# Two of sixteen low halves of the probabilities, made by GpSimd instead of VectorE, in a two-layer cross-attention kernel

## The chip, the cores and the metric

The kernel runs on one core of a Trainium2 chip. The metric is the device time of one execution in microseconds (us), lower is better. The engines are named as in the profile: PE is TensorE (PEld its weight loads), DVE is VectorE, ACT is ScalarE, POOL is GpSimd, SP is SyncE, which here only starts DMA transfers.

## The reference

The input x has 8 batches of 512 rows and 512 columns. It goes through two layers. Each layer adds to x a cross-attention over 77 context rows, and then a feed-forward product, each on a layer-normalised x.

```
x = x + xattn0(layernorm(x), ctx, mask)     # 16 heads of 32, softmax over 77 keys
x = x + ffn0(layernorm(x))                  # rows quantised to 8 bits, ternary weights
x = x + xattn1(layernorm(x), ctx)           # 16 heads of 64, output projection Wo
x = x + ffn1(layernorm(x))                  # FFT, sparse product, inverse FFT: one 512x512 matrix
```

Inside an attention:

```
scores = einsum('bhqd,bhkd->bhqk', q, k) / sqrt(HD)
probs = softmax(scores, axis=-1)
ctx = einsum('bhqk,bhkd->bqhd', probs, v)
```

## The kernel before

Every value that a matmul reads is kept as two fp16 numbers, a high half (the value rounded) and a low half (what the rounding left), and a product is made of three matmuls (lines 150 to 152). After a setup of about 195 us the batches go through a software pipeline: iteration i runs in 18 slots, and within it the stages work on different batches. Stage X is the first layer's attention (batch i), Y the second layer's attention (batch i-1), Z its output projection and second feed-forward (batches i-2, i-3), W the queries of the next batch. In the steady state an iteration takes 114 us.

An attention is cut into 8 units of 128 rows by 8 heads. X units 0 to 7 have their scores in slots 0 to 7, Y units 0 to 7 in slots 10 to 17, so slots 8 and 9 have no unit of their own. A unit that belongs to slot u goes on as follows. In slot u DVE takes the row maxima (`maxima`), ACT the exponential (`exp`), in fp32, into the tile `pr`. In slot u+1 DVE makes the reciprocals of the sums (`sums`, tile `sm`), and POOL multiplies `pr` by them in place (`normalise`, line 939). In slot u+2 ACT writes the high half, 256 times `pr`, in fp16 into the tile `ph` (`probs_high`, line 995), DVE writes the low half, 256 times `pr` minus the high half, beside it (`probs_low`, line 1156), and SP starts the transposing DMA of both into `prT` (`turn`), which PE reads for the product with the values. For X unit 6 that is slot 8 and for X unit 7 slot 9.

Each engine has its own list of work, written slot by slot in the same order, and meets the others by semaphores alone. Within a slot the orders are:

- DVE: maxima, sums of the unit before, the low halves of what PE's fills left in PSUM (`low`: `lo_part` at lines 1086 and 1088, `add_to` at line 1095 with the layernorm sums), `probs_low`, in slot 8 the layernorm sums of the next batch (`ln0`, lines 1037 to 1053), and then what the table `LOWER` lists: `quantise` or `rows_low`. In slot 9 that is `quantise` of layernorm 1 (lines 1062 to 1070), which makes the 8-bit rows of the first feed-forward.
- ACT: the high halves of the fills (line 963), `probs_high`, what `APPLY` lists (`ln_apply`, lines 1007 and 1010), `exp`. In slot 10 that is `ln_apply` of layernorm 3. It writes the buffers `xh` and `xn` and so waits until the last DVE step of `quantise` of slot 9 (line 1070) is done.
- POOL: `normalise`, then `rstd_of` for every layernorm group whose sums end in this slot (lines 930 and 932; in slot 8 that of `ln0`, which waits for DVE's line 1053), then what `BIAS` lists (`add_bias`, two additions at line 945). In slot 7 and in slot 10 there is such a pair.
- SP: `turn`, `turn_rows`, then stores and loads; in slot 8 four loads of `k0b` stand behind the `turn` of X unit 6.
- PE: in each slot the scores of the next unit, then the fills. In slots 8 to 11 these are the queries of Y (`project`), the value products of X rows 2 and 3, and the first feed-forward product. The scores of Y unit 2 wait for the exponential of Y unit 0.

The units in `HEADWISE` (X 7 and Y 0 among them) get their sums from ACT's exponential, so DVE's `sums` is for them the reciprocal alone.

Of the kernel before, what the change touches and what calls it, by code (L numbers as in the profile page):

```python
# [24 lines left out]
CH = (GK + 2) // 3  # L25
# [81 lines left out]
LN0_STATS = 8  # L107
HEADWISE = {("X", 0), ("X", 2), ("X", 5), ("X", 7), ("Y", 0), ("Y", 2), ("Y", 3), ("Y", 5)}
ROWS_BY_DVE = {(2, 2)}
APPLY = {2: [(2, 2)], 8: [(1, 0)], 10: [(3, 0)], 11: [(0, 0)], 12: [(0, 2)], 13: [(1, 2)], 14: [(3, 2)], 16: [(2, 0)]}  # L110
LOWER = {2: [(2, 2)], 9: [(1, 0)], 10: [(3, 0)], 11: [(0, 0)], 12: [(0, 2)], 13: [(1, 2)], 15: [(3, 2)], 17: [(2, 0)]}
BIAS = {7: [(2, 2)], 10: [(1, 0)], 12: [(3, 0)], 14: [(1, 2)], 17: [(2, 0), (3, 2)]}
# [22 lines left out]
def listed(table, g):  # L135

    i, s = SLOTS[g]
    out = [(j, pair, i - ln_lag(j, pair)) for j, pair in table.get(s, [])]
    return [e for e in out if there(e[2])]
# [602 lines left out]
def layers(nc, k, x, scr_k0, scr_k1, scr_v0, scr_v1, out):  # L742

    here = ExitStack()
    with here:
# [164 lines left out]
        def _(pool):  # L910
# [13 lines left out]
            def rstd_of(j, t0, width, b):  # L924
                n = GROUPS[j, b, t0]
                ts = slice(t0, t0 + width)
                pool.wait_ge(ln_var, n + 1)
                if b > 0:
                    pool.wait_ge(ln_applied, APPLIED[j, t0 + width - 2, b - 1] + 1)
                pool.tensor_tensor(rstd[:, j, ts], var[:, j, ts], mhalf[:, ts], ALU.pow).then_inc(rstd_ready, 1)  # L930
                pool.wait_ge(rstd_ready, n + 1)
                pool.tensor_tensor(shift[:, j, ts], mean[:, j, ts], rstd[:, j, ts], ALU.mult).then_inc(ln_ready, 1)  # L932

            def normalise(stage, u, b):
                U = UNIT[stage, u, b]
                pool.wait_ge(sums_ready, U + 1)
                v = pr[U % 3][:, :, 0:GK].rearrange("p g (h n) -> p g h n", h=4)
                s = sm[:, U % 4, :].rearrange("p (g h u) -> p g h u", g=2, u=1).broadcast_to([P, 2, 4, KEYS])
                pool.tensor_tensor(v, v, s, ALU.mult).then_inc(probs_ready, 1)  # L939

            def add_bias(j, pair, b):
                pool.wait_ge(ln_lowered if (j, pair) in ROWS_BY_DVE else ln_applied, APPLIED[j, pair, b] + 1)
# [5 lines left out]
            for g, (i, s) in enumerate(SLOTS):  # L948
                if unit_at(g - 1):
                    normalise(*unit_at(g - 1))  # L950
                for e in groups_at(g):
                    rstd_of(*e)
                for e in listed(BIAS, g):
                    add_bias(*e)

        @block.scalar
        def _(act):
# [31 lines left out]
            def probs_high(stage, u, b):  # L989
                U = UNIT[stage, u, b]  # L990
                act.wait_ge(probs_ready, U + 1)
                if U >= 2:
                    before = [v for v in UNIT if UNIT[v] == U - 2][0]
                    act.wait_ge(turned[before[1]], 16 * (PASS[before] + 1))
                act.activation(ph[:, U % 2, 0, :, :, 0:CH], pr[U % 3][:, :, 0:GKP].rearrange("p g (c n) -> p g c n", c=3), ACT.Copy,  # L995
                               scale=PS).then_inc(probs_hi, 1)

            def ln_apply(j, pair, b):
                n = APPLIED[j, pair, b]
# [32 lines left out]
        def _(dve):  # L1032
# [113 lines left out]
            def sums(stage, u, b):  # L1146
                U = UNIT[stage, u, b]
                dve.wait_ge(exp_done, U + 1)
                if (stage, u) not in HEADWISE:
                    step(dve.tensor_reduce(sm[:, U % 4, :].rearrange("p (g h) -> p g h", g=2), four(pr[U % 3][:, :, 0:GK]), AX.X, ALU.add))  # L1150
                dve.reciprocal(sm[:, U % 4, :], sm[:, U % 4, :]).then_inc(sums_ready, 1)  # L1151

            def probs_low(stage, u, b):
# [12 lines left out]
            for g, (i, s) in enumerate(SLOTS):  # L1166
# [3 lines left out]
                    sums(*unit_at(g - 1))  # L1170
                for use in SLOT_DRAINS[g]:
                    low(use)
                if unit_at(g - 2):
                    probs_low(*unit_at(g - 2))
                if s == LN0_STATS and there(i + 1):
                    ln0(i + 1)
# [205 lines left out]
```

## Time and profile before

| | us |
|---|---|
| median of 3 runs | 1245.94 (1243.89 to 1248.01) |
| the profiled execution, its own time | 1248.5 |
| its span, first to last instruction | 1246.7 |
| busy in it: PE | 975.0 (78%) |
| busy in it: DVE | 949.6 (76%) |
| busy in it: ACT | 647.6 (52%) |
| busy in it: POOL | 401.9 (32%) |

The span covers the setup, the pipeline's filling and emptying, and the iterations between. A share of busy time says little here: the stages have different limits, and what counts is, in each stretch, which engine is waited for last. "Idle before" at the end of a row is how long the engine stood before this instruction, and which instruction's end let it go on. Instruction ends on PE are modelled, and rows on POOL are rough.

### The profile page before, as it was taken

To read this page: it belongs to the slowest core of one execution; us is meant where nothing else is said; L and a number is where in the kernel's file an instruction comes from. 1 tells how busy PE (TensorE), PEld (TensorE's weight loads), DVE (VectorE), ACT (ScalarE), POOL (GpSimd) and SP (SyncE) were. 2 spreads that over 40 slices of the span, in tenths; PEclk is the share of its full clock that TensorE was granted. 3 is DMA by queue.
4 is the path that set the end of the run, shared out by engine and by line. 5 is a ranking of instruction groups with operands and counts; after the bars stand their busy time and mean duration, and the time that the engine had idled before them with its cause. 6 is when DMAs were issued, how large, how long until landed. Compare 5 with 4: busy or idle time off the path is not lost. (4 is left out here: it accounts for less than half of the span.)

```text
span 1246.7 us, 17114 instructions
## 1 busy us (share of the span) xinstructions
PE 975.0 (78%) x6020; PEld 511.7 (41%) x6020; DVE 949.6 (76%) x1740; ACT 647.6 (52%) x1658; POOL 401.9 (32%) x351
## 2 busy tenths in 40 slices
PE   3989950455587796999699879969996998789694
PEld 1446430232254343445345444444453444335341
DVE  5798973286879969987996999699888968944722
ACT  1334340363657648754964686387548646613701
POOL 0011004041433334523442444345234424511402
PEclk9999985756788798999899979989997999699797
DMA  9412332163555565575658465755745563550512
GB/s 343 164 34 70 115 119 91 34 128 68 90 114 109 102 115 93 108 133 114 110 103 155 76 121 102 150 100 99 140 106 115 101 119 65 113 102 17 106 47 68
DMA packets 374983, 132.83 MB, mean 107 GB/s; under 512 B 364753, under 2 KB 367345, under 8 KB 371442
## 3 DMA queue, kind: packets, MB, share of 16 engines
q1 hardware_dynamic: 374898, 131.74, 50.1%
q8 instruction: 48, 0.79, 0.3%
q14 instruction: 37, 0.30, 0.1%
HBM read 35.91 MB, written 16.11 MB: 42 GB/s over the span
## 5 line engine op out<-in xcount | busy, mean ns | idle before, releaser
L939 POOL TENSOR_TENSOR pr<-pr,sm 128x616 f32<-128x616 f32 x128 | 169.3, 1322 | 449.7 <-DVE sm L1151 449.7
L982 ACT ACTIVATE pr<-scores,mx,factor 128x77 f32<-128x77 f32 x512 | 203.9, 419 | 42.9 <-DVE mx L1139 42.8
L150 PE MATMUL wb<-xT,wq_hl 128*128 128x512 f16 x384 | 150.8, 393 | 68.1 <-DMA xT<-xh 68.1
L151 PE MATMUL wb<-xT,wq_hl 128*128 128x512 f16 x384 | 150.3, 391 | 0.0
L152 PE MATMUL wb<-xT,wq_hl 128*128 128x512 f16 x384 | 149.5, 389 | 0.0
L995 ACT ACTIVATE ph<-pr 128x618 f16<-128x618 f32 x128 | 92.6, 723 | 103.0 <-DMA prT<-ph 90.2
L150 PE MATMUL scores<-k1b,qc 128*128 128x154 f16 x256 | 62.5, 261 | 88.8 <-ACT pr L982 88.0
L1156 DVE SCALAR_TENSOR_TENSOR ph<-pr,ph 128x618 f16<-128x618 f32 x128 | 125.9, 983 | 3.7 <-ACT ph L995 3.7
L930 POOL TENSOR_TENSOR rstd<-var,mhalf 128x2 f32<-128x2 f32 (+1 forms) x48 | 52.6, 1096 | 179.9 <-DVE var L1053 172.8
L982 ACT ACTIVATION_READ_ACCUMULATOR pr<-scores,mx,factor 128x1 f32 x512 | 107.2, 209 | 0.0
L1136 DVE TENSOR_REDUCE mx<-scores 128x8 f32<-128x616 f32 x128 | 101.3, 791 | 6.3 <-PE scores L152 6.1
L150 PE MATMUL wb<-wo_hl,qc 128*128 128x512 f16 x256 | 97.0, 379 | 7.1 <-DVE qc L1086 6.8
L152 PE MATMUL wb<-wo_hl,qc 128*128 128x512 f16 x256 | 97.0, 379 | 0.0
L151 PE MATMUL wb<-wo_hl,qc 128*128 128x512 f16 x256 | 97.0, 379 | 0.0
L1079 DVE TENSOR_TENSOR xh<-xn,xh 128x1024 f16<-128x1024 f32 x48 | 73.4, 1530 | 30.4 <-ACT xn L1010 30.0
L1095 DVE SCALAR_TENSOR_TENSOR xr<-wb,factor,xr 128x512 f32<-128x512 f32 x48 | 35.7, 744 | 76.9 <-PE wb L152 76.9
L1007 ACT ACTIVATE xh<-xr,shift,rstd 128x512 f16<-128x512 f32 x72 | 57.9, 812 | 56.0 <-POOL shift L932 33.3
L150 PEld LDWEIGHTS wb<-xT,wq_hl 128*128 128x128 f16 x384 | 38.8, 101 | 114.0 <-issue 74.5
L963 ACT ACTIVATE qc<-wb,bq_s 128x512 f16<-128x512 f32 x64 | 42.3, 686 | 79.6 <-PE wb L152 79.6
L1010 ACT ACTIVATE xn<-xr,shift,rstd 128x512 f32<-128x512 f32 x84 | 66.9, 810 | 11.7 <-POOL shift L932 10.3
L945 POOL TENSOR_TENSOR xr<-xr,bf_b 128x512 f32<-128x512 f32 x48 | 69.9, 1476 | 3.8 <-ACT xn L1010 3.8
L1224 PE MATMUL scores<-mrow,ones 128*128 128x308 bf16 x128 | 42.0, 328 | 36.0 <-ACT pr L982 32.4
(178 smaller groups left out, 2571.6 us busy)
## 6 DMA issues: line engine op xcount, KB each, us to landing
xr<-in_x SPq DMA_DIRECT2D x6, 1024.0 KB, 5.7
out_x<-xr SPq DMA_DIRECT2D x6, 1024.0 KB, 5.4
a_dft_kf<-in_dft SPq DMA_DIRECT2D x1, 3072.0 KB, 14.2
a_stage<-in_wk SPq DMA_DIRECT2D x3, 1024.0 KB, 5.7
a_stage<-in_wv SPq DMA_DIRECT2D x3, 1024.0 KB, 5.6
scr_v<-a_wq_vs SPq DMA_DIRECT2D x1, 2560.0 KB, 7.8
scr_k<-a_wo_ks SPq DMA_DIRECT2D x1, 2464.0 KB, 7.2
k1b<-scr_k SPq DMA_DIRECT2D x16, 154.0 KB, 6.7
```

Source lines behind the costliest of these rows:

```text
L150: pe.matmul(out, lhs(0), rhs(0), start=start, stop=False, **kw)
L151: pe.matmul(out, lhs(0), rhs(1), start=False, stop=False, **kw)
L152: return pe.matmul(out, lhs(1), rhs(0), start=False, stop=stop, **kw)
L939: pool.tensor_tensor(v, v, s, ALU.mult).then_inc(probs_ready, 1)
L945: ins = pool.tensor_tensor(xs(b)[:, t, :], xs(b)[:, t, :], k[bias][:, :], ALU.add)
L982: ins = act.activation(pr[U % 3][:, h // 4, cols], sc[:, U % 2, h // 4, cols], ACT.Exp, bias=mx[:, U % 4, h:h + 1], scale=k["factor"][:, f ...
L995: act.activation(ph[:, U % 2, 0, :, :, 0:CH], pr[U % 3][:, :, 0:GKP].rearrange("p g (c n) -> p g c n", c=3), ACT.Copy, scale=PS).then_inc( ...
L1007: ins = act.activation(xh[:, n % 2, t - pair, 0, :], xs(b)[:, t, :], ACT.Identity, bias=shift[:, j, t:t + 1], scale=rstd[:, j, t:t + 1])
L1010: ins = act.activation(xn[:, t - pair, :], xs(b)[:, t, :], ACT.Identity, bias=shift[:, j, t:t + 1], scale=rstd[:, j, t:t + 1])
L1079: dve.tensor_tensor(xh[:, n % 2, :, 1, :], xn[:, :, :], xh[:, n % 2, :, 0, :], ALU.subtract).then_inc(ln_lowered, 1)
L1136: step(dve.tensor_reduce(m, s, AX.X, ALU.max))
L1156: dve.scalar_tensor_tensor(out=ph[:, U % 2, 1, :, :, 0:CH], in0=pr[U % 3][:, :, 0:GKP].rearrange("p g (c n) -> p g c n", c=3), scalar=PS, ...
```

## The change

The set `LOW_BY_POOL` names X units 6 and 7. For these two:

- DVE no longer runs `probs_low`; POOL runs it, in the same slot (8 and 9), behind `normalise` and `rstd_of` and ahead of `add_bias`. POOL's form is a plain subtraction without the factor 256.
- The factor moves: DVE divides the sums by 256 ahead of the reciprocal (a tensor_scalar on 128x8, with a wait between the two), so that `pr` comes out of `normalise` 256 times as large, and ACT's `probs_high` uses the scale 1.
- `rstd_of` gets a further wait on DVE's `ln_lowered` of the batch before, for the second group of layernorm 2.

```diff
+LOW_BY_POOL = {("X", 6), ("X", 7)}
...
                 pool.wait_ge(ln_var, n + 1)
                 if b > 0:
                     pool.wait_ge(ln_applied, APPLIED[j, t0 + width - 2, b - 1] + 1)
+                    for pair in range(t0, t0 + width, 2):
+                        if (j, pair) in ROWS_BY_DVE:
+                            pool.wait_ge(ln_lowered, APPLIED[j, pair, b - 1] + 1)
...
+            def probs_low(stage, u, b):
+                U = UNIT[stage, u, b]
+                pool.wait_ge(probs_hi, U + 1)
+                pool.tensor_tensor(ph[:, U % 2, 1, :, :, 0:CH], pr[U % 3][:, :, 0:GKP].rearrange("p g (c n) -> p g c n", c=3),
+                                   ph[:, U % 2, 0, :, :, 0:CH], ALU.subtract).then_inc(probs_lo, 1)
...
                 for e in groups_at(g):
                     rstd_of(*e)
+                if unit_at(g - 2) and unit_at(g - 2)[:2] in LOW_BY_POOL:
+                    probs_low(*unit_at(g - 2))
                 for e in listed(BIAS, g):
                     add_bias(*e)
...
                 act.activation(ph[:, U % 2, 0, :, :, 0:CH], pr[U % 3][:, :, 0:GKP].rearrange("p g (c n) -> p g c n", c=3), ACT.Copy,
-                               scale=PS).then_inc(probs_hi, 1)
+                               scale=1.0 if (stage, u) in LOW_BY_POOL else PS).then_inc(probs_hi, 1)
...
                     step(dve.tensor_reduce(sm[:, U % 4, :].rearrange("p (g h) -> p g h", g=2), four(pr[U % 3][:, :, 0:GK]), AX.X, ALU.add))
+                if (stage, u) in LOW_BY_POOL:
+                    step(dve.tensor_scalar(sm[:, U % 4, :], sm[:, U % 4, :], 1.0 / PS, None, ALU.mult))
                 dve.reciprocal(sm[:, U % 4, :], sm[:, U % 4, :]).then_inc(sums_ready, 1)
...
-                if unit_at(g - 2):
+                if unit_at(g - 2) and unit_at(g - 2)[:2] not in LOW_BY_POOL:
                     probs_low(*unit_at(g - 2))
```

POOL in slots 7 to 10 of one iteration, before. `pr<-pr,sm` is `normalise` of X unit 7, the rows on 128x4 are `rstd_of` for `ln0`, `bf_b` is the bias that `add_bias` adds.

```order
L945 TENSOR_TENSOR xr<-xr,bo_b 128x512
L939 TENSOR_TENSOR pr<-pr,sm 128x2x308 [waits sums_ready]
L930 TENSOR_TENSOR rstd<-var,mhalf 128x4 [waits ln_applied,ln_var]
L932 TENSOR_TENSOR shift<-mean,rstd 128x4 [waits rstd_ready]
L945 TENSOR_TENSOR xr<-xr,bf_b 128x512 [waits ln_applied]
L945 TENSOR_TENSOR xr<-xr,bf_b 128x512
```

The same place after:

```order
L955 TENSOR_TENSOR xr<-xr,bo_b 128x512
L943 TENSOR_TENSOR pr<-pr,sm 128x2x308 [waits sums_ready]
L934 TENSOR_TENSOR rstd<-var,mhalf 128x4 [waits ln_applied,ln_var]
L936 TENSOR_TENSOR shift<-mean,rstd 128x4 [waits rstd_ready]
L948 TENSOR_TENSOR ph<-pr,ph 128x6x103 [waits probs_hi] x2
L955 TENSOR_TENSOR xr<-xr,bf_b 128x512 [waits ln_applied]
L955 TENSOR_TENSOR xr<-xr,bf_b 128x512
```

Both low halves now stand one behind the other between `rstd_of` and the two additions.

DVE from the end of slot 7 to `quantise` in slot 9, before. `ph<-pr,ph` are `probs_low` of X units 5, 6 and 7, and `amax`, `cscale`, `ascale` belong to `quantise`.

```order
L1156 SCALAR_TENSOR_TENSOR ph<-pr,ph 128x6x103 [waits probs_hi]
L1151 RECIPROCAL sm<-sm 128x8 [waits exp_done]
L1088 SCALAR_TENSOR_TENSOR qc<-wb,bq_s,qc 128x512 [waits bank_hi]
L1156 SCALAR_TENSOR_TENSOR ph<-pr,ph 128x6x103 [waits probs_hi]
L1037 BN_STATS stats<-x 128x6 [waits x_loaded]
...
L1053 TENSOR_TENSOR var<-var,half 128x4 [waits dve_step]
L1088 SCALAR_TENSOR_TENSOR qc<-wb,bq_s,qc 128x512 [waits bank_hi] x3
L1156 SCALAR_TENSOR_TENSOR ph<-pr,ph 128x6x103 [waits probs_hi]
L1062 TENSOR_REDUCE amax<-xn 128x2 [waits rows_turned0,ln_applied]
L1063 TENSOR_SCALAR amax<-amax 128x2 [waits dve_step]
```

The same place after:

```order
L1170 SCALAR_TENSOR_TENSOR ph<-pr,ph 128x6x103 [waits probs_hi]
L1164 TENSOR_SCALAR sm<-sm 128x8 [waits exp_done]
L1165 RECIPROCAL sm<-sm 128x8 [waits dve_step]
L1100 SCALAR_TENSOR_TENSOR qc<-wb,bq_s,qc 128x512 [waits bank_hi]
L1049 BN_STATS stats<-x 128x6 [waits x_loaded]
...
L1065 TENSOR_TENSOR var<-var,half 128x4 [waits dve_step]
L1100 SCALAR_TENSOR_TENSOR qc<-wb,bq_s,qc 128x512 [waits bank_hi] x3
L1074 TENSOR_REDUCE amax<-xn 128x2 [waits rows_turned0,ln_applied]
L1075 TENSOR_SCALAR amax<-amax 128x2 [waits dve_step]
```

Two low halves have gone, and a small tensor_scalar stands ahead of the reciprocal of X unit 7.

## Rows read from the trace of the kernel before

**Rows 1.** Waits, whole run: who waited for whom, us in total, times, longest.

```profile
ACT xh L1007 <- DVE xh L1070: 19.5, 6, 3.7
```

**Rows 2.** Waits of PE from 706 to 820 us.

```profile
PE scores L150 <- ACT pr L982: 11.8, 3, 6.6
```

**Rows 3.** Timeline of ACT, slots 9 and 10: start, duration, instruction, idle before.

```profile
810.53 0.69 ACT L963 ACTIVATE qc<-wb,bq_s 128x512 f16<-128x512 f32 x1 [1.81 <-PE wb L152]
811.12 0.71 ACT L995 ACTIVATE ph<-pr 128x618 f16<-128x618 f32 x1
...
817.14 0.81 ACT L1007 ACTIVATE xh<-xr,shift,rstd 128x512 f16<-128x512 f32 x1 [3.33 <-DVE xh L1070]
```

**Rows 4.** Timeline of DVE, slots 8 and 9 of the same iteration.

```profile
804.44 0.19 DVE L1151 RECIPROCAL sm<-sm 128x8 f32<-128x8 f32 x1
...
805.17 0.79 DVE L1156 SCALAR_TENSOR_TENSOR ph<-pr,ph 128x618 f16<-128x618 f32 x1
...
808.46 1.22 DVE L1048 TENSOR_TENSOR half<-stats 128x4 f32<-128x4 f32 x1
...
810.20 2.06 DVE L1088 SCALAR_TENSOR_TENSOR qc<-wb,bq_s,qc 128x512 f16<-128x512 f32 x3
812.18 1.36 DVE L1156 SCALAR_TENSOR_TENSOR ph<-pr,ph 128x618 f16<-128x618 f32 x1
813.46 1.21 DVE L1062 TENSOR_REDUCE amax<-xn 128x2 f32<-128x1024 f32 x1
...
815.44 0.88 DVE L1068 TENSOR_SCALAR xn<-xn,ascale 128x512 f32<-128x512 f32 x2
816.36 0.69 DVE L1070 TENSOR_SCALAR xh<-xn 128x1024 bf16<-128x1024 f32 x1
```

**Rows 5.** Timeline of POOL, slots 7 to 10 of the same iteration.

```profile
803.89 1.19 POOL L930 TENSOR_TENSOR rstd<-var,mhalf 128x2 f32<-128x2 f32 x1 [0.97 <-DVE var L1053]
...
805.97 2.51 POOL L945 TENSOR_TENSOR x<-x,bo_b 128x512 f32<-128x512 f32 x2
808.43 1.23 POOL L939 TENSOR_TENSOR pr<-pr,sm 128x616 f32<-128x616 f32 x1
810.36 1.02 POOL L930 TENSOR_TENSOR rstd<-var,mhalf 128x4 f32<-128x4 f32 x1 [0.71 <-DVE var L1053]
...
811.61 3.06 POOL L945 TENSOR_TENSOR xr<-xr,bf_b 128x512 f32<-128x512 f32 x2
```

**Rows 6.** Single lines of code: duration ns min/median/max, first and last start.

```profile
L939 POOL TENSOR_TENSOR pr<-pr,sm x128: 1208/1217/1775, 248.4 to 1179.0; 128x616 f32<-128x616 f32 x128
L945 POOL TENSOR_TENSOR xr<-xr,bf_b x48: 1257/1270/2302, 358.5 to 1229.6; 128x512 f32<-128x512 f32 x48
L1139 DVE TENSOR_SCALAR mx<-mx,factor x64: 230/231/415, 244.6 to 1163.7; 128x8 f32<-128x8 f32 x64
```

**Rows 7.** Timelines of POOL and DVE where their instructions meet.

```profile
717.68 3.05 POOL L945 TENSOR_TENSOR xr<-xr,bf_b 128x512 f32<-128x512 f32 x2
718.34 1.26 DVE L1156 SCALAR_TENSOR_TENSOR ph<-pr,ph 128x618 f16<-128x618 f32 x1
719.52 2.28 DVE L1079 TENSOR_TENSOR xh<-xn,xh 128x1024 f16<-128x1024 f32 x1
...
296.37 1.11 DVE L1064 TENSOR_SCALAR cscale<-amax,factor 128x2 f32<-128x2 f32 x1
```

**Rows 8.** Timelines of POOL and ACT in iterations 0 and 1, of PE in iteration 4.

```profile
278.13 3.04 POOL L945 TENSOR_TENSOR x<-x,bf_b 128x512 f32<-128x512 f32 x2
277.24 0.72 ACT L995 ACTIVATE ph<-pr 128x618 f16<-128x618 f32 x1 [2.08 <-DMA prT<-ph]
283.47 0.81 ACT L1007 ACTIVATE xh<-xr,shift,rstd 128x512 f16<-128x512 f32 x1 [5.35 <-issue]
366.17 0.42 ACT L982 ACTIVATE pr<-scores,mx,factor 128x77 f32<-128x77 f32 x1 [3.74 <-DVE mx L1139]
709.16 0.24 PE L150 MATMUL scores<-k1b,qc 128*128 128x154 f16 x1 [1.30 <-ACT pr L982]
```

## The prediction, made before the changed kernel ran

> **What bounds the kernel now.** I read first the waits of the whole run, then the timelines of all engines through one iteration of the steady state, slots 7 to 14. PE is 78% busy and DVE 76%, and neither share tells what sets the length of an iteration. In the list of waits the reader should look for an engine that waits for DVE and for which PE then waits. That is ACT: in six iterations it stands before `ln_apply` of layernorm 3 until DVE has finished `quantise`, 19.5 us in all, 3.3 us each time [rows 1, 3]. From 817.14 on ACT works almost without a gap for 23 us, through four `ln_apply` and the exponentials of Y units 0 to 3, and PE waits for exactly those exponentials, 11.8 us in one iteration in three waits [rows 2]. Behind them PE is nearly gapless up to the queries of the next slots 7 to 9, whose last high half ACT writes at 810.53 to 811.22 [rows 3] and DVE's three low halves follow [rows 4]. So the loop closes over DVE's slots 8 and 9: **the moment at which `quantise` ends (816.36 + 0.69 = 817.05) moves the whole iteration one for one**, earlier by up to the 3.3 us that ACT waits, later without a limit. In iteration 1 it is DVE's maxima right behind `quantise` that ACT waits for, 3.74 us [rows 8]; in iteration 0 ACT's 283.47 stands right behind `quantise` too. That makes eight iterations.
>
> **How DVE and POOL meet.** The second thing to see is that some instructions of DVE and of POOL exclude each other. POOL begins two additions at 717.68, 1.26 us each when alone [rows 6]. DVE's low half, 0.79 us when alone (805.17, [rows 4]), starts at 718.34 and takes 1.26: it waits for the first addition. The pair takes 3.05 instead of 2.5: the second addition waits for the low half. DVE's next instruction starts at 719.52, while the low half is finishing, and still takes 2.28, some 1.06 more than its 1.22 alone: it waits for the second addition [rows 7]. So they take turns: **each such DVE instruction lets one waiting POOL instruction pass and is then held by the next for its whole length.** Small ones are held too: 1.11 us for a tensor_scalar on two columns at 296.37 [rows 7], 1.22 for one of `ln0`'s at 808.46 under POOL's `normalise` [rows 4, 5]. Reductions, reciprocals and what reads PSUM run on (813.46 takes its 1.21 under POOL's 811.61 to 814.67; the three from 810.20 pass under 810.36 [rows 4, 5]).
>
> **What goes from DVE.** Sixteen low halves go. Of X unit 6 it is 805.17 to 805.88, 0.7 us; of X unit 7 it is 812.18 to 813.46, 1.3 us, since today it is held by the bias addition [rows 4, 5].
>
> **What comes to DVE.** One tensor_scalar with a wait for each unit, by its like 0.23, of which some 0.2 shows [rows 6]. For unit 6 it lies in slot 7, where DVE waits for PE some 2 us behind it, and costs nothing. For unit 7 it takes the reciprocal's place at 804.44, inside POOL's 803.89 to 805.08 [rows 4, 5], and so ends near 805.25: 0.8 later for all behind it. With unit 6's 0.7 gone, the layernorm sums start 0.1 later than now. POOL in turn, no longer held by unit 6's low half, starts its additions at 805.4 instead of 805.97 and ends `normalise` of unit 7 at 809.1 instead of 809.66, and `ln0` ends 0.5 earlier, at 809.7. The third of the query low halves must wait for ACT's 811.22 in any case and ends at about 811.95 (before: 812.26). `quantise` thus starts at 811.9 instead of 813.46: 1.55 us earlier.
>
> **What comes to POOL.** Two subtractions on 128x618, of a kind that no row shows. From below the nearest is `normalise`, 616 columns with a broadcast operand, 1.22 us; the other is the bias addition, two full operands, 1.26 for 512 columns, by columns 1.52 us [rows 6]. I take 1.5, since two full operands are what the subtraction has. As an upper end I take 1.9: the addition costs 2.46 ns a column and `normalise` 1.98, 1.24 times as much, and mixing fp16 in may add as much again. The Trainium skill (GPSIMD Engine Reference, § Elementwise, side-by-side cycle accounting) gives 2.6 cycles per element at 1.2 GHz for a two-input operation, by estimate 1.34 us for 618 before its dispatch; no row here shows it, and by it the sum below would be some 2 us smaller.
>
> **Where the subtractions land.** Before, POOL is free from 811.5 but for the two additions, which end at 814.67 just as DVE's reduction (813.46 to 814.67) does, so that none of `quantise`'s six following tensor_scalars is held [rows 4, 5]. After, with the 1.5:
>
> - POOL is through with `rstd_of` at about 811.2, subtracts unit 6 to 812.7 and unit 7 (its high half is there at 811.83 [rows 3]) to 814.2, and then adds the biases.
> - DVE's reduction runs from 811.9 to 813.15. L1063 comes under the subtraction of unit 7: held to 814.2, done 814.35.
> - First addition 814.35 to 815.6. L1064 is held by it: done 815.75.
> - Second addition 815.75 to 817.0. L1066 is held by it: done 817.15.
> - L1068 twice and L1070, with POOL idle, take 1.6 now, from 815.44 to 817.05 [rows 4]: done near 818.7.
>
> That is 817.05 before, about 818.7 after: **1.6 us later an iteration** in place of 1.55 earlier. With 1.22 for the subtraction it is 1.15 later, with 1.9 it is 2.5 later.
>
> In iteration 0 POOL is free for the first subtraction at 278.13 [rows 8]. Unit 7's follows to 281.1, the additions end at 284.15, and the same three holds put `quantise`'s end at 285.8, against 283.4 now (ACT's 283.47): 2.4 us (1.9 and 3.1 at the ends). PE's value product waits there for unit 7's transpose, which moves by as much.
>
> **The sum:** 7 x 1.6 + 2.4 = 13.6 us. The profiled execution took 1248.5, so 1262.1; it lies 2.6 above the median of the runs shown, 1245.94, so I forecast **1259.5**. With the ends of the subtraction's price: 7 x 1.15 + 1.9 = 10 gives 1256, 7 x 2.5 + 3.1 = 20.6 gives 1266.5.
>
> **What costs nothing, and its cover.** SP's `turn` of unit 6 moves from 805.9 to 812.7, and the four loads of `k0b` and the `turn` of unit 7 queue behind it; the last starts some 3 us later than now, at 816.5, and its data are wanted only by the third-next fill of PE, after 820.8, which itself moves by 1.6. If that cover fell short, PE's wait for Y unit 0's exponential still stands behind it. The bias pair ends at 817 instead of 814.7 and is wanted by DVE 14 us later. The further wait of `rstd_of` is for a step a whole iteration old. ACT's scale costs the same at 1 as at 256.
>
> **Rivals.**
>
> 1. *One hold fewer.* A small tensor_scalar may slip in where one POOL instruction ends and the next begins; L1063 did so just ahead of the row at 296.37 [rows 7]. That saves one addition, 1.25 us, each time: 0.35 x 7 + 1.15 = 3.6 us, **1249.5**. Against it: in the row at 719.52 DVE's instruction was ready at the boundary and lost it. It decides by whether the reduction ends within 0.1 us of a POOL end, and I put that at 813.15, in the middle of a subtraction.
> 2. *No collision: faster.* If the subtraction doesn't hold `quantise`'s small instructions as the addition does, or POOL is through so early that they run free, the 1.55 us is won: 7 x 1.55 + 0.5 = 11.4 us, **1234.5**. It needs POOL's four instructions out of the way by 813.2, when by any price above they end at 816 or later; or an exclusion that is different for this form. For it speaks only that no row shows the form.
> 3. *PE's clock falls earlier.* PE waits 1.3 us for Y unit 0's exponential now [rows 8] and would wait 2.9. If that took its clock from the upper level to the lower for the twelve matmuls behind (0.22 us each at the upper, 0.43 at the lower), it would cost 2.6 us more an iteration: 13.6 + 18, **1278**. Waits of 6.6 us are followed by the lower level today, the one of 1.3 isn't.
>
> **How the numbers follow.** Full collision 0.68, one hold fewer 0.14 (it straddles the bound: 0.09 the same, 0.05 slower), no collision 0.14, clock 0.04. A measurement of this kernel can tell about 0.3% (3.7 us) from no change. So faster 0.14, same 0.09, slower 0.77. The range must leave out no more than 2 in 10: it takes in the full collision with both prices (1256 to 1266.5) and the case with one hold fewer, with some room on both sides, 1243 to 1268, and leaves out 1234.5 and 1278.
>
> **What would show it right or wrong.** In slots 8 and 9 of the changed trace: the small tensor_scalar on `sm` of X unit 7 at 0.7 us or more; the reduction of `quantise` about 1.5 us earlier relative to the last query; the rows of L1063, L1064 and L1066's successors at 1.1 us or so instead of 0.17 to 0.23; POOL's subtraction at 1.5; ACT's wait for `quantise` near 5 us instead of 3.3, and PE's first wait near 2.9 instead of 1.3. If the small instructions keep their 0.17 and ACT's wait shrinks to some 1.8, the collision step is wrong and the time falls. If the wait grows and the time doesn't, the step from `quantise` to the iteration's length is.

## The result, and the profile after

| | before | after |
|---|---|---|
| median beside each other, 6 runs each, us | 1246.80 (1243.23 to 1248.21) | 1253.95 (1250.98 to 1256.46) |
| ratio, 95% interval | | 1.0066 (1.0050 to 1.0083) |
| profiled execution, its own time | 1248.5 | 1250.98 |
| its span | 1246.7 | 1249.2 |

The changed kernel is slower by 7.2 us. It ran once more later, beside 23 runs of the kernel before on one chip, and came out at 1.0057 (1.0039 to 1.0076). The two spans alone would give only 2.5 us, and that is chance in two places. The row of POOL's `rstd` for `ln0` (128x4) stands at one place of each iteration and serves as a mark. In the fourteen profiles of this case the first mark used lies anywhere from 274.0 to 278.3 us, and the stretch from the last mark used to one more such row takes either 85.1 to 85.6 or 87.0, whatever the kernel. The execution profiled after, the shortest of its runs, had an early start and a short end. From mark to mark:

```profile
276.89 1.01 POOL L930 TENSOR_TENSOR rstd<-var,mhalf 128x4 f32<-128x4 f32 x1 [2.11 <-DVE var L1053]
357.23 1.02 POOL L930 TENSOR_TENSOR rstd<-var,mhalf 128x4 f32<-128x4 f32 x1 [1.03 <-DVE var L1053]
468.36 1.02 POOL L930 TENSOR_TENSOR rstd<-var,mhalf 128x4 f32<-128x4 f32 x1 [0.71 <-DVE var L1053]
923.92 1.02 POOL L930 TENSOR_TENSOR rstd<-var,mhalf 128x4 f32<-128x4 f32 x1 [0.71 <-DVE var L1053]
1029.82 1.01 POOL L930 TENSOR_TENSOR rstd<-var,mhalf 128x4 f32<-128x4 f32 x1 [3.29 <-DVE var L1053]
1131.79 1.01 POOL L930 TENSOR_TENSOR rstd<-var,mhalf 128x4 f32<-128x4 f32 x1 [36.27 <-DVE var L1053]
```

Those are the marks of the kernel before (timeline of POOL: start, duration, instruction, idle before), and these the ones of the changed kernel:

```profile
274.56 1.01 POOL L934 TENSOR_TENSOR rstd<-var,mhalf 128x4 f32<-128x4 f32 x1 [1.61 <-DVE var L1065]
358.27 1.02 POOL L934 TENSOR_TENSOR rstd<-var,mhalf 128x4 f32<-128x4 f32 x1 [0.79 <-DVE var L1065]
469.69 1.02 POOL L934 TENSOR_TENSOR rstd<-var,mhalf 128x4 f32<-128x4 f32 x1 [0.78 <-DVE var L1065]
928.86 1.02 POOL L934 TENSOR_TENSOR rstd<-var,mhalf 128x4 f32<-128x4 f32 x1 [0.79 <-DVE var L1065]
1035.48 1.01 POOL L934 TENSOR_TENSOR rstd<-var,mhalf 128x4 f32<-128x4 f32 x1 [3.08 <-DVE var L1065]
1136.81 1.01 POOL L934 TENSOR_TENSOR rstd<-var,mhalf 128x4 f32<-128x4 f32 x1 [34.58 <-DVE var L1065]
```

| stretch between two marks, us | before | after | difference |
|---|---|---|---|
| iteration 0 | 80.34 | 83.71 | +3.4 |
| iteration 1 | 111.13 | 111.42 | +0.3 |
| iterations 2 to 5, each | 113.89 | 114.79 | +0.90, four times 3.6 |
| iteration 6, first part | 105.90 | 106.62 | +0.7 |
| the stretch behind it, with iteration 7's `quantise` | 101.97 | 101.33 | -0.6 |
| all | 854.90 | 862.25 | +7.4 |

So 7.4 us lie between the marks, as much as between the medians. The step that repeats is +0.9 us an iteration, and it is seen in slots 8 to 10 of the iteration at 815 us. On POOL, which answers to [rows 5]:

```profile
815.59 2.60 POOL L948 TENSOR_TENSOR ph<-pr,ph 128x618 f16<-128x618 f32 x2
818.15 2.49 POOL L955 TENSOR_TENSOR xr<-xr,bf_b 128x512 f32<-128x512 f32 x2
```

DVE in the same stretch, which answers to [rows 4]; lines 1074 to 1082 are `quantise`:

```profile
809.02 0.16 DVE L1164 TENSOR_SCALAR sm<-sm 128x8 f32<-128x8 f32 x1
...
815.83 0.75 DVE L1100 SCALAR_TENSOR_TENSOR qc<-wb,bq_s,qc 128x512 f16<-128x512 f32 x1 [0.24 <-ACT qc L975]
816.50 1.21 DVE L1074 TENSOR_REDUCE amax<-xn 128x2 f32<-128x1024 f32 x1
817.74 0.47 DVE L1075 TENSOR_SCALAR amax<-amax 128x2 f32<-128x2 f32 x1
818.25 1.19 DVE L1076 TENSOR_SCALAR cscale<-amax,factor 128x2 f32<-128x2 f32 x1
...
819.54 1.12 DVE L1078 TENSOR_SCALAR ascale<-ascale 128x2 f32<-128x2 f32 x1
820.70 0.88 DVE L1080 TENSOR_SCALAR xn<-xn,ascale 128x512 f32<-128x512 f32 x2
821.61 0.69 DVE L1082 TENSOR_SCALAR xh<-xn 128x1024 bf16<-128x1024 f32 x1
```

Three instructions on two columns take 0.47, 1.19 and 1.12 us. The first ends with the second subtraction, the second with the first bias addition, the third with the second addition at 820.64. Over the whole run the same shows in the groups by line (x: count, busy us in total, mean ns). Before:

```profile
L1063 DVE TENSOR_SCALAR amax<-amax 128x2 f32<-128x2 f32 x16 | 3.8, 234 | 0.6
L1064 DVE TENSOR_SCALAR cscale<-amax,factor 128x2 f32<-128x2 f32 x16 | 4.5, 284 | 0.6
L1066 DVE TENSOR_SCALAR ascale<-ascale 128x2 f32<-128x2 f32 x16 | 2.7, 169 | 0.6
L1068 DVE TENSOR_SCALAR xn<-xn,ascale 128x512 f32<-128x512 f32 x32 | 14.1, 484 | 0.6
```

After:

```profile
L1075 DVE TENSOR_SCALAR amax<-amax 128x2 f32<-128x2 f32 x16 | 4.2, 265 | 0.6
L1076 DVE TENSOR_SCALAR cscale<-amax,factor 128x2 f32<-128x2 f32 x16 | 12.1, 759 | 0.6
L1078 DVE TENSOR_SCALAR ascale<-ascale 128x2 f32<-128x2 f32 x16 | 10.4, 651 | 0.6
L1080 DVE TENSOR_SCALAR xn<-xn,ascale 128x512 f32<-128x512 f32 x32 | 16.1, 544 | 0.6
```

These four lines grew by 0.4, 7.6, 7.7 and 2.0, in all 17.7 us of standing still, as much as the sixteen low halves were worth (line 1156 had 125.9 us with 128 of them; line 1170 has 109.4 with 112). And they stand in `quantise`, for which ACT waits: 23.7 us over the whole run in place of 19.5 [rows 1].

```profile
ACT xh L1019 <- DVE xh L1082: 23.7, 6, 4.0
```

ACT in this iteration of the changed kernel, which answers to [rows 3]:

```profile
815.11 0.69 ACT L975 ACTIVATE qc<-wb,bq_s 128x512 f16<-128x512 f32 x1 [1.90 <-PE wb L153]
...
822.39 0.81 ACT L1019 ACTIVATE xh<-xr,shift,rstd 128x512 f16<-128x512 f32 x1 [4.01 <-DVE xh L1082]
```

DVE's low half of the third query stands right ahead of `quantise` and waits for ACT's high half. Measured from that ACT row, `quantise` ends 7.19 us later (815.11 to 821.61 + 0.69); before it was 6.52 (810.53 to 817.05). The mean over iterations 2 to 5 went from 6.60 to 7.20, so 0.6 of the 0.9 us lies here. The other 0.3 lies between the end of `quantise` and the same ACT row of the next iteration, 107.28 us before and 107.59 after; the experiments below say what it is not, but no run names it. PE's first wait for Y unit 0's exponential, a little later (timeline of PE):

```profile
828.54 0.24 PE L151 MATMUL scores<-k1b,qc 128*128 128x154 f16 x1 [1.99 <-ACT pr L994]
```

Before, this wait was 1.30 us [rows 8], and 1.31 in this same iteration: +0.68, the same shift again.

Behind this longer wait the clock of PE falls, in this iteration and in iteration 2 of the changed kernel; in the kernel before it falls behind this wait in none. Windows of equal length from just before the end of the wait, before and after (PE busy is the second number with its matmuls, PEclk the third from the end):

```profile
823.15:826.75 3.60, 3.46 (x25) 2.05 (x26) 3.04 (x6) 3.60 (x7) 1.22 (x1) 1.00 0.61 115
828.40:832.00 3.60, 3.46 (x18) 2.06 (x19) 3.04 (x6) 3.60 (x7) 1.22 (x1) 0.56 0.62 116
```

In the same busy time PE did 18 matmuls in place of 25, at 0.56 of full speed on average, most of it at the lower level, 1.2 GHz. Little comes of it, since PE soon has to wait for ACT again, and the slower matmuls take up a part of that next wait (timelines of PE, before and after):

```profile
835.12 0.31 PE L150 MATMUL scores<-k1b,qc 128*128 128x154 f16 x1 [6.59 <-ACT pr L982]
841.15 0.31 PE L151 MATMUL scores<-k1b,qc 128*128 128x154 f16 x1 [5.70 <-ACT pr L994]
```

From the mark, PE comes out of this wait at 26.81 us where the clock fell early and at 26.03 in iterations 3, 4 and 6, where it didn't, and out of the wait after that at 31.99 and 31.67. At the end of the iteration no difference is left to see: the two with the early fall took 114.75 and 114.51 us from mark to mark, the two between them 114.59 and 115.31.

### The profile page after: what moved, and what is told of

Its sections match the earlier page's. It is cut to its first block and busy times, and to the rows that moved or that the text cites. A ratio compares the mean times of both kernels' runs of the same rounds, so it can differ in the third digit from the quotient of the medians.

```text
span 1249.2 us, 17130 instructions
## 1 busy us (share of the span) xinstructions
PE 970.3 (78%) x6020; PEld 509.5 (41%) x6020; DVE 955.0 (76%) x1740; ACT 648.3 (52%) x1658; POOL 415.6 (33%) x367
## 5 line engine op out<-in xcount | busy, mean ns | idle before, releaser
L1170 DVE SCALAR_TENSOR_TENSOR ph<-pr,ph 128x618 f16<-128x618 f32 x112 | 109.4, 977 | 2.7 <-ACT ph L1007 2.6
```

What stands on the lines that cost most here:

```text
L1170: dve.scalar_tensor_tensor(out=ph[:, U % 2, 1, :, :, 0:CH], in0=pr[U % 3][:, :, 0:GKP].rearrange("p g (c n) -> p g c n", c=3), scalar=PS, ...
```

## The experiments

The theory is that the change loses its time because POOL's two subtractions push its two bias additions of slot 10 under DVE's `quantise`, whose small instructions they hold. The rivals were that the scaling step on DVE costs it, that the transposes and loads on SP come late, or that POOL's total work is what slows DVE. All runs below stand in three sets; within a set all kernels ran on one chip, beside the same runs of the kernel before.

**The scale alone.** DVE makes all low halves again; the scale stays in the sums, and the further wait stays on POOL.

```diff
-                if unit_at(g - 2) and unit_at(g - 2)[:2] in LOW_BY_POOL:
-                    probs_low(*unit_at(g - 2))
...
-                                         scalar=PS, in1=ph[:, U % 2, 0, :, :, 0:CH], ...
+                                         scalar=1.0 if (stage, u) in LOW_BY_POOL else PS, in1=ph[:, U % 2, 0, :, :, 0:CH], ...
...
-                if unit_at(g - 2) and unit_at(g - 2)[:2] not in LOW_BY_POOL:
+                if unit_at(g - 2):
```

> One part alone: the factor 256 moves into the reciprocal for X units 6 and 7 (the two small tensor_scalars on DVE, ACT's scale 1), but both low halves stay on DVE. Theory (the loss comes from where POOL's two subtractions land, the small DVE instruction itself is worth 0.2 us an iteration): 1.4 us slower than before, ratio 1.001. Rival (the added step ahead of the reciprocal, with its wait, is what costs): about 8 us slower than before, ratio 1.0065, like the full change.

Measured: ratio 1.0001 (0.9985 to 1.0017), 854.9 us between the outer marks as before. The scaling step costs nothing that shows (an iteration takes 113.97 us where it took 113.89); the loss lies in who makes the low halves.

**The bias pair waits for the end of `quantise`.** In the changed kernel, POOL's two additions of slot 10 wait for a later semaphore, the one that DVE raises when it has finished line 1082. Nothing else in the program changes.

```diff
-                pool.wait_ge(ln_lowered if (j, pair) in ROWS_BY_DVE else ln_applied, APPLIED[j, pair, b] + 1)
+                pool.wait_ge(ln_lowered if (j, pair) in ROWS_BY_DVE | {(1, 0)} else ln_applied, APPLIED[j, pair, b] + 1)
```

> The changed kernel, with one wait exchanged: POOL's pair of bias additions of slot 10 waits until DVE has finished quantise, so that it can't lie under quantise's small instructions. Theory of the collision: L1076 and L1078 fall back to 0.17 to 0.23 us, quantise ends 1.7 us earlier an iteration than in the changed kernel, ACT's wait for it falls from 4.0 to about 2.3 us; iteration 0 keeps its 3.4 us. Sum 7 x (0.7 - 1.7) + 3.4 = 4 us faster than before, ratio 0.997. Rival (unit 7's probabilities come too late to PE because POOL makes them): the time stays where it is, about 8 us above before, ratio 1.0065.

Measured: 0.9978 (0.9962 to 0.9995), and once more on another chip 0.9976 (0.9961 to 0.9991). Its POOL and DVE, in the iteration at 812 us:

```profile
811.23 2.60 POOL L948 TENSOR_TENSOR ph<-pr,ph 128x618 f16<-128x618 f32 x2
816.12 2.50 POOL L955 TENSOR_TENSOR xr<-xr,bf_b 128x512 f32<-128x512 f32 x2 [2.28 <-DVE xh L1082]
...
813.37 0.49 DVE L1075 TENSOR_SCALAR amax<-amax 128x2 f32<-128x2 f32 x1
813.89 0.23 DVE L1076 TENSOR_SCALAR cscale<-amax,factor 128x2 f32<-128x2 f32 x1
...
814.22 0.17 DVE L1078 TENSOR_SCALAR ascale<-ascale 128x2 f32<-128x2 f32 x1
```

The two holds by the additions are gone (0.23 and 0.17 instead of 1.19 and 1.12); the rest of the subtraction still holds line 1075. One wait on POOL turns +7.2 us into -4.3 and, on the other chip, -2.5. `quantise` now ends 5.30 us after its ACT row, 1.9 earlier than in the changed kernel, and an iteration is 1.9 us shorter. So the collision is the cause, shown by taking it away alone. What it doesn't explain is the 0.3 us in the rest of the loop, from `quantise`'s end to the next ACT row: that stretch is 107.57 us here, as in the changed kernel, and 107.2 to 107.3 in the kernel before, with the scale alone and in the next experiment. It comes with the move of the low halves and stays when nothing collides.

**The same wait in the kernel before.** The same edit, without the change.

> The kernel before with the same exchanged wait alone. Theory of the collision: the low half of X unit 7 on DVE falls from 1.36 to 0.8 us, quantise ends 0.6 us earlier an iteration, 7 x 0.6 = 4 us faster than before, ratio 0.9965. Rival (the end of quantise doesn't set the iteration's length one for one): no change, ratio 1.000.

Measured: 0.9984 (0.9969 to 1.0000), and on the other chip 0.9976 (0.9961 to 0.9991). That is between what the two expected in the first run, which alone can't exclude no change, and nearer to the theory in the second: the pair of the kernel before, too, holds something that counts, DVE's low half of X unit 7 [rows 4]. It takes 0.79 now in place of 1.36, and the iterations come down from 113.89 to 113.26 us.

**Does the move gain anything once nothing collides?** The second set repeated both with the loads on SP put first (below), the third repeated the two themselves, and the changed kernel with them.

> The changed kernel itself once more, beside the three below on one chip. It was at 1.0066 in its own comparison, while two variants of it, one with 2.2 us less in iteration 0 and one with nothing less between the marks, came out at 1.0035 and 1.0046 beside another set of runs. Theory (the marks in the trace tell the truth and the sets of runs differ by 0.1 to 0.2%): 1.005 to 1.0066. Rival (the change costs less than the first comparison showed): 1.003 to 1.004.

> The changed kernel with the wait before the bias pair of slot 10. Theory: steady part 667 to 668 against 672.6 in the kernel before, ratio 0.997 to 0.998, and 0.1% below the kernel before with the same wait. Rival (moving the low halves is worth nothing even with the collision gone): level with the kernel before with the same wait.

> The kernel before with the same wait. Theory: 0.998 to 0.999, since its bias pair holds two later instructions less than in the changed kernel and the wait frees the low half of unit 7 alone. Rival (the wait is all that gains in both): the same ratio as the changed kernel with the wait, 0.997 to 0.998.

| between marks, us | iteration 0 | iteration 1 | 2 to 5, each | ratio |
|---|---|---|---|---|
| before | 80.3 | 111.1 | 113.89 | 1 |
| after | 83.7 | 111.4 | 114.79 | 1.0066 |
| after, again | 84.1 | 112.0 | 114.82 | 1.0057 |
| after, pair waits | 83.3 | 111.4 | 112.86 | 0.9978 |
| the same, again | 84.6 | 112.0 | 112.90 | 0.9976 |
| before, pair waits | 81.5 | 110.1 | 113.26 | 0.9984 |
| the same, again | 81.9 | 110.1 | 113.22 | 0.9976 |

In each of the steady iterations POOL's low halves then gain 0.3 to 0.4 us, and iterations 0 and 1 take 1.8 to 2.7 and 1.2 to 1.9 us back. Between the outer marks the move thus costs 0.2 us with the wait on one chip (851.9 against 851.6) and 2.0 on the other (853.9 against 851.9), where it costs 7.4 without the wait. The ratios can't tell the two kernels apart. The theory had the changed kernel 0.1% ahead; these runs don't show it.

**The queue on SP.** In iteration 0 the changed kernel lost 3.4 us, and X unit 7's transpose stood behind four loads. SP and PE of the changed kernel in iteration 0:

```profile
278.63 2.39 SPq L842 DMA_DIRECT2D k0b<-scr_k  x4
281.06 1.44 SPq L864 DMA_TRANSPOSE prT<-ph  x1
...
285.12 0.21 PE L151 MATMUL wb<-v0b,prT 103*128 103x64 f16 x1 [7.62 <-DMA prT<-ph]
```

First the loads were put a slot later:

```diff
-                if s == 8 and there(i + 1) and i + 1 > 0:
+                if s == 9 and there(i + 1) and i + 1 > 0:
                     load_k(0, i + 1)
```

> The changed kernel with SP's four loads of k0b moved from slot 8 to slot 9, behind the transposes of unit 7 and of the quantised rows. Theory (iteration 0 lost 3.4 us because unit 7's transpose stood behind unit 6's, which now waits for POOL, and behind these loads; PE waited 7.6 us for it instead of 4.0): iteration 0 gets 2.4 us back and the rest stays, 5.5 us slower than before, ratio 1.0045. Rival (iteration 0's loss is the collision alone): no change against the changed kernel, about 8 us slower than before, ratio 1.0065, PE's wait still near 7.6 us.

Measured: 1.0062 (1.0047 to 1.0076), nearer to the rival's number. Iteration 0 came down from 83.7 to 82.0 us, with PE's wait at 5.33 us in place of 7.62, but iteration 1 went up from 111.4 to 112.8 and the others from 114.79 to 114.96, so nothing is left of it in all. Then they were put ahead of unit 6's transposes:

```diff
+                if s == 8 and there(i + 1) and i + 1 > 0:
+                    load_k(0, i + 1)
                 if unit_at(g - 2):
                     turn(*unit_at(g - 2))
...
-                if s == 8 and there(i + 1) and i + 1 > 0:
-                    load_k(0, i + 1)
```

> The changed kernel, with SP's four loads of the next k0b in slot 8 issued ahead of the transposes of unit 6 instead of between those of unit 6 and unit 7. Theory: in iteration 0 of the changed kernel unit 7's transpose stood behind these loads on SP (they were issued from 278.63 to 281.02 us, the transpose at 281.06), which is about 1 us of the 3.4 us that iteration 0 lost; the steady iterations don't feel it. With the loads first, iteration 0 (before 80.3, changed kernel 83.7 between the two marks) comes to 82 to 83, the steady part stays at 677, and the ratio to the kernel before is 1.005 to 1.006. Rival: the queue on SP was not what iteration 0 waited for: 83.7 and 1.0066 again.

> The changed kernel with SP's four loads of k0b ahead of unit 6's transposes. Theory: some 2 us less than the changed kernel on the same chip (iteration 0 at 81.5 instead of 83.7 between the marks, nothing elsewhere), so its ratio is 0.0015 to 0.002 below. Rival: the 2.2 us were chance in one profile, and the two are level within 0.0005.

Measured: 1.0035 (1.0021 to 1.0049), and in the third set 1.0048 (1.0029 to 1.0067) where the changed kernel itself had 1.0057. SP in the first of these runs, where the transposes now follow one another:

```profile
274.77 2.37 SPq L842 DMA_DIRECT2D k0b<-scr_k  x4
279.46 3.31 SPq L864 DMA_TRANSPOSE prT<-ph  x2
```

Iteration 0 takes 81.5 and 82.0 us instead of 83.7 and 84.1, and iteration 1 some 0.6 to 0.8 more than there; 1.4 to 1.9 us in all between the outer marks. The third set's two ratios differ by 0.0009, between what its theory (0.0015 to 0.002) and its rival (within 0.0005) expected, and their intervals overlap. By the marks the queue on SP is thus a second, small part of the loss, in iteration 0 only; the times alone don't show it. That order, the wait, and both kernels:

> The changed kernel, with both: the bias pair of slot 10 waits for the end of the quantising step, and SP issues the loads of k0b ahead of unit 6's transposes. Theory: the steady part as with the wait alone (667.3, before 672.6), and iteration 0 some 1 us shorter than the 83.3 there; ratio 0.997. Rival: the loads first delay something of unit 6 on SP that the wait alone has not, and the ratio is back at 0.998 to 1.000.

> The kernel before with the same two edits. Theory: the loads make no difference where VectorE makes the low halves, so this is the wait alone again: iteration 0 at 81 to 81.5 us (80.3 without it), steady part 668.3, ratio 0.998 to 0.999, and so the move of the low halves to GpSimd, once nothing of GpSimd's stands in the way of the quantising step, is worth 0.1 to 0.2% (the run with both edits on the changed kernel at 0.997). Rival: the move as such is what gains in those kernels, and this one stays at 1.000.

Measured: the changed kernel with both 0.9951 (0.9933 to 0.9968), the kernel before with both 0.9973 (0.9961 to 0.9985). Their intervals overlap a little; beside each other on one chip the medians are 1241.81 and 1243.81 us, and between the outer marks they have 852.3 and 853.6. So here the changed kernel is ahead by 0.1 to 0.2%, as the last expectation has it; with the wait alone the other two sets don't confirm it. The kernel before had 854.9, so the 0.5% of the changed kernel with both is more than its own marks show (0.2%), and 0.2 to 0.3% is what the marks and the runs with the wait alone support. It has the lowest median measured, but the wait alone had 851.9 and 853.9 between the marks, so what the order of the loads adds to the wait isn't shown.

**Whole instructions, or columns?** The bias additions of slot 10 cut in two, in the changed kernel: four of 256 columns in place of two of 512.

```diff
+                cuts = (0, 256, 512) if (j, pair) == (1, 0) else (0, 512)
                 for t in (pair, pair + 1):
-                    ins = pool.tensor_tensor(xs(b)[:, t, :], xs(b)[:, t, :], k[bias][:, :], ALU.add)
+                    for lo, hi in zip(cuts, cuts[1:]):
+                        ins = pool.tensor_tensor(xs(b)[:, t, lo:hi], xs(b)[:, t, lo:hi], k[bias][:, lo:hi], ALU.add)
```

> The changed kernel, with GpSimd's two bias additions of slot 10 cut into four of 256 columns each: the same columns in total. Theory (a VectorE instruction is held until the GpSimd instruction in progress ends, whole instructions in turn): the holds on the copy of the xh pieces and on the subtraction of the xh pieces shorten from 1.2 and 1.1 us to about 0.7 each, two later instructions may be held by 0.6 instead; the quantising step ends 0.3 to 0.8 us earlier in each iteration, steady part 672 to 675 in place of 677.2, ratio 1.002 to 1.005. Rival (it is the total of GpSimd's columns that slows VectorE, whatever their cut): 677 to 678, since four instructions cost a little more than two, ratio 1.0066 to 1.008.

The two holds that the expectation names by pieces of `xh` are those of the `cscale` and `ascale` lines, L1076 and L1078 of the changed kernel. POOL and DVE with the cut (two lines further down in this kernel's numbering):

```profile
819.97 2.96 POOL L957 TENSOR_TENSOR xr<-xr,bf_b 128x256 f32<-128x256 f32 x4
...
820.07 0.65 DVE L1078 TENSOR_SCALAR cscale<-amax,factor 128x2 f32<-128x2 f32 x1
...
820.82 0.58 DVE L1080 TENSOR_SCALAR ascale<-ascale 128x2 f32<-128x2 f32 x1
821.44 1.77 DVE L1082 TENSOR_SCALAR xn<-xn,ascale 128x512 f32<-128x512 f32 x2
```

Each hold is now half as long, 0.65 and 0.58 us, and the scaling of the two rows, which ran free before (0.88), takes 1.77 since two more pieces hold it. So a hold lasts as long as what is left of the piece of POOL's work in progress. But there are more of them: `quantise`'s four lines have 40.5 us over the run against 42.8 in the changed kernel, and it ends 7.02 us after its ACT row against 7.20, less than the 0.3 to 0.8 expected. A period is 114.58 against 114.79, iterations 1 to 6 together (the "steady part" of the expectation) 676.7 against 677.2, where the theory had 672 to 675 and the rival 677 to 678, and all between the outer marks 864.2 against 862.2. The ratio is 1.0046 (1.0027 to 1.0066), in the theory's range, but it isn't told apart from 1.0057 and 1.0066. The holds are as the theory has them, the gain in time is as the rival has it: nearly nothing, because what one hold saves the further ones take. What counts is how much of POOL's work lies under `quantise`.

A kernel with one unit alone on POOL was not run, so how the loss divides between the two units stays open.

## Why the prediction was right, and by how much it missed

The direction and the chain held; the size was too large. It forecast 13.6 us, 7 times 1.6 and 2.4, and 7.2 were measured. The median of 1253.95 lies below the 1256 to 1266.5 that the prediction worked out for the full collision; it is inside the stated range by the room that was left for the case of one hold fewer, and that case is not what made the time short. That much is luck.

- **POOL's order and the start of `quantise`: right.** The reduction was to start 1.37 us after ACT's third query half (811.9 against 810.53); it starts 1.39 after it (816.50 against 815.11).
- **Three holds, at L1063, L1064 and L1066: right** in iterations 2 to 6, one for one, and their ends are POOL's ends. In iterations 1 and 7 the first of them didn't occur. That is the first rival, which the prediction judged by where the reduction ends: in these iterations the second subtraction starts late, since it waits for ACT's high half, and at 1.32 us it ends 0.1 after the reduction (363.61 and 363.51 in iteration 1), so that the small instruction slips in ahead of the first addition:

```profile
363.54 0.17 DVE L1075 TENSOR_SCALAR amax<-amax 128x2 f32<-128x2 f32 x1
```

It saves 0.36 us (`quantise` takes 5.45 in place of 5.81 from its first row on), not the 1.25 that the rival had, since both additions still hold the next two. The rival with no hold did not come about.
- **The price of the subtraction: mis-sized.** 1.5 us was taken, 1.32 is the median of the sixteen. Twice 0.18 is 0.36 us an iteration.

```profile
L948 POOL TENSOR_TENSOR ph<-pr,ph x16: 1318/1322/1328, 275.8 to 1045.8; 128x618 f16<-128x618 f32 x16
```

The lower end of the range, by `normalise`'s 1.22, was nearer than the value taken; two full operands and fp16 add 0.1, not 0.3. The Trainium skill (GPSIMD Engine Reference, § Elementwise, side-by-side cycle accounting) gave an estimate of 1.34 before dispatch, and this row agrees with it to 0.02, with no dispatch to be seen on top.

- **POOL held by DVE's small instructions: wrong.** The step let each of DVE's small instructions between two additions delay POOL by 0.15 us, so that the pair ended 6.47 us after the query half. The pair takes 2.49, as if alone, and ends 5.53 after it: of the 0.94 between, 0.36 are the subtractions, 0.2 an earlier start, and the rest is this step. `quantise` ends 7.19 after the query half where 8.17 was forecast.
- **From `quantise` to the iteration: right, within 0.3 us.** ACT's wait grew by 0.7 and PE's by 0.68, with +0.67 in `quantise`; forecast were ACT near 5 and PE near 2.9, with the oversized step. Over iterations 2 to 5 `quantise` ends 0.60 later after its ACT row and the iteration is 0.90 longer; with the wait on POOL it is 1.30 earlier and 1.03 shorter, and in the kernel before with the wait 0.56 earlier and 0.63 shorter. Between the marks iterations 1 to 6 come to 4.6 us, where six times 1.6 is 9.6: 5.0 of the 6.2 us by which the sum of 13.6 is above the 7.4. Iteration 1 alone lost 0.3 (in the second profile of the changed kernel, 112.0 us, it is 0.9); why so little stays open.
- **Iteration 0: 2.4 forecast, 3.4 measured, and by another path.** The prediction had three holds put the end of `quantise` 2.4 us later. There are four, each by one of POOL's four instructions, and on other lines: L1076 and L1078 by the subtractions (1.24 and 1.18 us), the two parts of L1080 by the additions, 2.84 us for the pair instead of 0.88.

```profile
278.36 2.66 POOL L955 TENSOR_TENSOR x<-x,bf_b 128x512 f32<-128x512 f32 x2
...
278.46 2.84 DVE L1080 TENSOR_SCALAR xn<-xn,ascale 128x512 f32<-128x512 f32 x2
```

But they hardly count there. With the pair out of the way `quantise` is 2.0 us shorter in iteration 0 (5.66 against 7.62 from its first row on), and the iteration only 0.4 (83.3 against 83.7). What PE waits for is the transpose of unit 7; first in the kernel before, then in the changed kernel with the pair waiting:

```profile
283.36 0.21 PE L150 MATMUL wb<-v0b,prT 103*128 103x64 f16 x1 [3.99 <-DMA prT<-ph]
286.99 0.21 PE L151 MATMUL wb<-v0b,prT 103*128 103x64 f16 x1 [7.48 <-DMA prT<-ph]
```

From the first mark that is 6.47 and 10.42 us; in the changed kernel itself it is 10.56 with a wait of 7.62. The prediction named this wait and let it move by its 2.4. What it left out is the `turn` of unit 7 behind the four loads, which it named as queued and costed at nothing for the steady state: moving the loads gave 2 us of iteration 0 back. In the steady iteration looked at here that cost of nothing is right, PE doesn't wait for a transpose in it.

- **Iteration 7: +1.6 forecast, -0.6 measured.** Up to ACT's row at 1102.26 it had lost 1.0 us since the mark: its distance from the mark is 66.78, and 65.74 before (1095.56). The next six microseconds give it back, with the clock. Windows from that row to ACT's next one, before and after (PE busy is the second number, PEclk the granted clock):

```profile
1095.56:1102.21 6.65, 4.26 (x16) 1.65 (x15) 4.12 (x6) 1.51 (x2) 0.00 (x0) 0.85 0.87 164
```

```profile
1102.26:1108.03 5.77, 3.39 (x16) 1.39 (x15) 4.13 (x6) 1.52 (x3) 0.00 (x0) 1.00 0.83 156
```

The same 16 matmuls took PE 4.26 us at a granted clock of 0.85 on average and 3.39 at 1.00, which is 2.4 GHz throughout. Before, a part of this stretch ran at the lower level, 1.2 GHz. That is 0.9 us, and the next step of ACT, 2.09 us before (1102.21 to 1104.30) and 1.29 after (1108.03 to 1109.32), is another 0.8, the same seven matmuls at 0.65 before and 1.00 after: 1.0 - 0.9 - 0.8 is the -0.6 and what rounding leaves. That the lower level fell elsewhere than on work in the changed kernel is what the rows show; why it did, no run here tells.

- **The small tensor_scalar on `sm`: cheaper than forecast.** 0.8 us were expected for unit 7's, under POOL's power on two columns; it took 0.16 there (809.02, with POOL's row 808.47 to 809.66). It saved nothing in the end, since `ln0`'s first instruction met `normalise` instead, as before, and took 1.13 at 812.45. The run with the scale alone shows the same, 1.0001.
- **The clock of PE: wrong that it stays up at this place, right that this costs nothing to speak of.** The third rival had it fall behind PE's first wait, if that wait grew to 2.9 us. It grew to 2.0 only, and the clock fell behind it in iterations 2 and 5, as the windows above show for the latter. It did so in two or three of the steady iterations in each of the five further profiles in which the additions stand under `quantise`, and in none of the eight others. The rival's price of 2.6 us an iteration didn't come: PE's later waits for ACT took the slower matmuls in. The mean over the run is 0.889 to 0.892 in the two profiles of the changed kernel and 0.884 in the one before.

## What to carry to other kernels

Work handed to GpSimd is paid for twice where its instructions, or those that it pushes back on GpSimd, come to lie beside short VectorE instructions in a chain that others wait for: here VectorE was freed of 16.5 us and stood still for 17.7. Look at what GpSimd would be doing during the chain, and let work that nobody wants yet wait until the chain is through; one later semaphore did more than the move of the work itself. When pricing holds, add up all of GpSimd's work that comes to lie under the chain, what is pushed back included, and not only the work that moved; cutting it into smaller instructions changed next to nothing here.

## What the runs showed of the hardware

- A VectorE tensor_scalar on two columns stands 1.1 to 1.2 us for a GpSimd addition of 512 columns (1.25 us) and 0.6 for one of 256 (0.74 us): a hold lasts to the end of the instruction in progress. The reduction on 1024 columns (1.21 us at 816.50, under two subtractions) and the reciprocals (0.15) were never held. One that started 0.07 us before the end of GpSimd's instruction slipped in ahead of the next (363.54 under a row that ends at 363.61; it took 0.17). The Trainium skill (SBUF — State Buffer, § Who interferes with whom) says of the port pair that the two engines share that whichever starts first has it for its whole instruction, that a tensor_scalar may need it, and that a tensor_reduce never does; these rows agree.
- By that rule every GpSimd instruction would hold for its whole length. Here the measurement decides: the last half microsecond of the power on 128x2 holds nothing. It takes 0.71 us by itself (at 307.88), and 1.19 where VectorE's low half of 0.80 began 0.16 ahead of it, so it waits for the low half and has some 0.55 left. In that rest, in the kernel before, a further low half starts at 272.75 and takes 0.81, as if alone, with the power's row at 272.06 to 273.25. The tensor_scalar on 128x8 of the changed kernel took 0.16 in the same place (809.02, under 808.47 to 809.66) in all eight iterations; since it starts within 0.1 us of the low half's end, it alone wouldn't show this.
- GpSimd's additions aren't longer for the small VectorE instructions between them: 2.49 us for the pair at 818.15, which is twice the shortest single one [rows 6], while the low half of 0.79 us lengthened a pair to 3.05 [rows 7].
